# Attention weights of a graph layer: made ahead in four stages, with sums on ScalarE and a shorter ELU

## What is computed

```python
h = x @ W
al = h @ a_l
ar = h @ a_r
e = jnp.exp(-jax.nn.leaky_relu(al[src] + ar[dst], negative_slope=NEG_SLOPE))
rowsum = jax.ops.segment_sum(e, src, num_segments=N)
h_prime = jax.ops.segment_sum(e[:, None] * h[dst], src, num_segments=N)
h_prime = h_prime / (rowsum[:, None] + EPS)
return jax.nn.elu(h_prime)
```

## Time and profile before

| | us |
|---|---|
| median of three runs | 1708.2 |
| lowest, highest | 1707.59, 1710.76 |
| the profiled execution's own time | 1708.83 |
| its span in the profile | 1707.0 |
| PE busy | 1574.6 |
| DVE, ACT, POOL busy | 936.9, 720.7, 341.9 |

### The profile page before, as it was taken

The page is one execution under the profiler, slowest core; times in us unless marked ns, Lnnn a source line. Parts: engine busy times, 40 slices in busy tenths (PEclk is TensorE's granted clock), DMA queues, the critical chain, the costliest instruction groups (busy, mean ns, idle before and its releaser), DMA issues.

```text
span 1707.0 us, 19694 instructions
## 1 busy us (share of the span) xinstructions
PE 1574.6 (92%) x7072; PEld 1255.8 (74%) x7072; DVE 936.9 (55%) x1457; ACT 720.7 (42%) x1246; POOL 341.9 (20%) x670
## 2 busy tenths in 40 slices
PE   4797999999999999999999998978976999999995
PEld 3676778888677877787878777766754778777774
DVE  8785778887645343323342435554466538633345
ACT  4355766767733333333332233343322224543233
POOL 4132012233311010101010102232345104401015
PEclk9999999999999999999999999989988899999998
DMA  4233234324674434333444244533434145545235
GB/s 150 73 85 134 72 97 159 101 69 130 227 256 163 141 122 158 122 128 96 151 146 134 86 130 167 203 120 135 119 106 140 65 153 178 209 167 182 86 110 166
DMA packets 101882, 232.04 MB, mean 136 GB/s; under 512 B 22967, under 2 KB 25902, under 8 KB 101776
## 3 DMA queue, kind: packets, MB, share of 16 engines
q1 hardware_dynamic: 87366, 182.92, 33.7%
q10 hardware_dynamic: 14410, 47.74, 7.6%
HBM read 171.24 MB, written 59.37 MB: 135 GB/s over the span
## 4 chain that ended last, share of the span: by engine, by line
PE 63%; DVE 16%; ACT 8%; POOL 5%; issue 5%; DMA 2%; ACTq 0%; DVEq 0%; SPq 0%; POOLq 0%
PE bank L744 12%; PE bank L746 12%; PE bank L745 12%; PE bank L861 10%; PE bank L872 6%; PE bank L865 4%; PE bank L863 4%; ACT Tt L1007 2%; DMA x_d<-XO 2%; ACT Mh L987 1%; PE bank L795 1%; DVE Tt L1246 1%; ACT XO L1064 1%; PE bank L927 1%; DVE Ml L1232 1%
## 5 line engine op out<-in xcount | busy, mean ns | idle before, releaser
L744 PE MATMUL bank<-wh,xh 128*125 128x512 f32 x1040 | 423.1, 407 | 18.2 <-issue 14.3
L861 PE MATMUL bank<-Zh,Mh 125*125 125x512 f32 x1000 | 406.5, 406 | 8.4 <-ACT Mh L996 3.6
L745 PE MATMUL bank<-wl,xh 128*125 128x512 f32 x1040 | 412.7, 397 | 0.0
L746 PE MATMUL bank<-wh,xl 128*125 128x512 f32 x1040 | 412.4, 397 | 0.0
L1218 DVE TENSOR_TENSOR xl<-xs,xh 128x1000 fp32r<-128x1000 f32 x120 | 147.0, 1227 | 290.3 <-ACT xh L970 290.3
L970 ACT CAST xh<-xs 128x1000 fp32r<-128x1000 f32 x130 | 133.0, 1025 | 301.9 <-PE bank L746 284.2
L744 PEld LDWEIGHTS bank<-wh,xh 128*125 128x125 f32 x1040 | 194.7, 187 | 67.8 <-issue 16.8
L872 PE MATMUL bank<-Zl,Mh 125*125 125x512 f32 x600 | 237.6, 396 | 0.0
L746 PEld LDWEIGHTS bank<-wh,xl 128*125 128x125 f32 x1040 | 194.9, 187 | 49.9
L861 PEld LDWEIGHTS bank<-Zh,Mh 125*125 125x125 f32 x1000 | 189.9, 190 | 55.8 <-issue 6.2
L745 PEld LDWEIGHTS bank<-wl,xh 128*125 128x125 f32 x1040 | 195.1, 188 | 44.6
(11 more groups left out here) (165 smaller groups left out, 2110.6 us busy)
## 6 DMA issues: line engine op xcount, KB each, us to landing
xs<-xT_d SPq DMA_DIRECT2D x80, 500.0 KB, 3.6
Ar<-a_d SPq DMA_DIRECT2D x100, 312.5 KB, 3.1
xs<-hT_d SPq DMA_DIRECT2D x40, 500.0 KB, 3.6
x_d<-XO ACTq DMA_DIRECT2D x30, 512.0 KB, 4.0
R<-x_d SPq DMA_DIRECT2D x60, 256.0 KB, 4.2
xT_d<-XT ACTq DMA_DIRECT2D x30, 500.0 KB, 2.7
ws<-in_W SPq DMA_DIRECT2D x34, 256.0 KB, 3.3
m_d<-Tt ACTq DMA_DIRECT2D x10, 625.0 KB, 4.5
```

The lines of the kernel that those rows point to most:

```text
L744: te.matmul(o, xh[i % 2][:, k, :], wh[s][:], start=(k == 0), stop=False)
L745: te.matmul(o, xh[i % 2][:, k, :], wl[s][:], start=False, stop=False)
L746: m = te.matmul(o, xl[i % 2][:, k, :], wh[s][:], start=False, stop=(k == 7))
L861: te.matmul(o, Mh[i][:, s, :], zh, start=(n == 0), stop=False)
```

## The change

- **A third T tile.** Matrix d uses tile d mod 3. The third tile is laid over the two `XO` buffers, joined into one. `t_release` now takes the job that had the tile before.
- **Four stages.** For att job i, the sums and the leaky ReLU come at the end of iteration i - 4 (`SUM_AT`), the exponential and `times` in iteration i - 3 (`EXP_AT`), `Mh`, `Ml` and the fold in i - 2, the product in i. Its `Ar` is loaded in i - 4.
- **Sums on ACT** instead of POOL: ten activations of 125 x 125 with a column of `PQ` as bias.
- **Row sums.** One fold on POOL, to five blocks; PE sums five blocks instead of three, ahead of product j rather than behind it, into bank 6 or 7 by turns. `row_scale` makes `RS` early in DVE's iteration j.
- **ELU with one hop**, in att and kept jobs: ACT takes relu and exp of the scaled product straight from PSUM, DVE then takes min(exp, 1) + relu, and adds R and -1 as before. ACT thereby waits for the product's end itself, and for the `U` tiles.
- **The store to `m_d`** goes from ACT's queue to SP's, in `late(j)` for matrix j + 2, ahead of the load of `R` for j. For att and kept jobs DVE's `Ml` of j + 2 now comes after the layer norm's small step `soon` instead of before it; both are ahead of `post`.

```diff
+SUM_AT, EXP_AT = {}, {}
...
     if _j > J0[0] + 1:
-        LOAD_AT.setdefault(_j - 3, []).append(_j)
+        LOAD_AT.setdefault(_j - (4 if _job.kind == "att" else 3), []).append(_j)
+    if _job.kind == "att":
+        SUM_AT[_j - 4], EXP_AT[_j - 3] = _j, _j
+ATT = [_j for _j, _job in enumerate(JOBS) if _job.kind == "att"]
...
+def t_slot(j):
+
+    if JOBS[j].kind == "gate":
+        return TI[j] % 2
+    return JOBS[j].d % (3 if JOBS[j].kind == "att" else 2)
...
+T_BEFORE = {j: next((i for i in reversed(TJ[:TI[j]]) if t_slot(i) == t_slot(j)), None) for j in TJ}
...
-        XF = [sb(f"XO{i}", [128, D], f32) for i in range(2)]
+        XB = sb("XO", [128, 2 * D], f32)
+        XF = [XB[:, i * D:(i + 1) * D] for i in range(2)]
         XO = [t[0:T, :] for t in XF]
+
+        T3 = [TF[0][:], TF[1][:], XB[:, 0:NT * T]]
+        Tt.append(XB[0:T, 0:NT * T].rearrange("p (a c) -> p a c", c=T))
...
             q.wait_ge(s_ml, m_done(j))
             if JOBS[j].kind == "att":
-                q.wait_ge(s_half, 2 * JOBS[j].d + 2)
-                q.wait_ge(d_t[t_slot(j)], 16 * (JOBS[j].d // 2 + 1))
+                q.wait_ge(s_half, JOBS[j].d + 1)
+                m_stored(q, j)
+
+        def m_stored(q, j):
...
+            d = JOBS[j].d
+            q.wait_ge(d_m[d % 3], 16 * (d // 3 + 1))
...
+                if j + 2 < NJ and JOBS[j + 2].kind == "att":
+                    o = j + 2
+                    q.wait_ge(s_mul, e_done(o))
+                    sy.dma_start(m_d[JOBS[o].d], T3[t_slot(o)]).then_inc(d_m[JOBS[o].d % 3], 16)
...
-                if job.kind == "att":
-                    d = job.d
-                    q.wait_ge(s_half, 2 * d + 2)
-                    if d:
-                        q.wait_ge(s_post, PI[j])
-                    q.wait_ge(s_te, sum(1 for o in range(j) for _ in GROUPS[o]))
...
-                        m = te.matmul(bank[7][0:T, 0:1], GW[0:T, d % 2, c * T:(c + 1) * T], ones[0:T, 0:1],
-                                      start=(c == 0), stop=(c == 4))
-                    m.then_inc(s_row, 1)
+
+            def row_sums(j):
+                d = JOBS[j].d
+                q.wait_ge(s_half, d + 1)
+                if d >= 2:
+                    q.wait_ge(s_rs, d - 1)
+                q.wait_ge(s_te, 3 * NT + 1 + sum(1 for o in range(j) for _ in GROUPS[o]))
+                for c in range(NT // 2):
+                    m = te.matmul(bank[6 + d % 2][0:T, 0:1], GW[0:T, d % 2, c * T:(c + 1) * T], ones[0:T, 0:1],
+                                  start=(c == 0), stop=(c == NT // 2 - 1))
+                m.then_inc(s_row, 1)
...
-                if job.kind == "att":
-                    ac.dma_start(m_d[job.d], TF[t_slot(j)][:]).then_inc(d_t[t_slot(j)], 16)
...
+            def sums(j):
+
...
+                if t_slot(j) == 2 and d == 2:
+                    for o in range(NT - 2, NT):
+                        q.wait_ge(s_tt, GROUPS[fin_of(1, o)][-1][0] + 1)
+                        x_stored(q, fin_of(1, o))
+                else:
+                    t_release(q, T_BEFORE[j])
+                for s in range(NT):
+                    m = ac.activation(t[:, s, :], PB[:, d, :], ACT.Identity, bias=PQ[0][0][:, s:s + 1])
+                m.then_inc(s_sum, 1)
+
+            def exps(j):
+                q.wait_ge(s_leak, JOBS[j].d + 1)
+                ac.activation(Tt[t_slot(j)], Tt[t_slot(j)], ACT.Exp, scale=-1.0).then_inc(s_exp, 1)
...
                 elif job.kind in ("att", "kept"):
-                    q.wait_ge(s_el, NT * job.half + d + 1)
-                    ac.activation(U[1], U[1], ACT.Exp).then_inc(s_elu, 1)
+                    q.wait_ge(s_mm, j + 1)
+                    q.wait_ge(s_rs, d + 1)
+                    u_free(q, j)
+                    p = bank[BANK[j]][0:T, :]
+                    ac.activation(U[0], p, ACT.Relu, scale=RS[:, d:d + 1]).then_inc(s_elu, 1)
+                    ac.activation(U[1], p, ACT.Exp, scale=RS[:, d:d + 1]).then_inc(s_elu, 1)
...
+                if j in EXP_AT:
+                    exps(EXP_AT[j])
...
+                if j in SUM_AT:
+                    sums(SUM_AT[j])
...
+            def row_scale(j):
+                d = JOBS[j].d
+                q.wait_ge(s_row, 2 + d + 1)
+                chain("v", ve.tensor_scalar(RS[:, d:d + 1], bank[6 + d % 2][0:T, 0:1], 1e-5, None, ALU.add))
+                mine()
+                ve.reciprocal(RS[:, d:d + 1], RS[:, d:d + 1]).then_inc(s_rs, 1)
...
-                    q.wait_ge(s_mm, j + 1)
-                    u_free(j)
-                    chain("v", ve.tensor_scalar(U[0], p, RS[:, d:d + 1], None, ALU.mult))
-                    mine()
-                    ve.tensor_scalar(U[1], U[0], 0.0, None, ALU.min).then_inc(s_el, 1)
-                    q.wait_ge(s_elu, NT * f + d + 1)
-                    chain("v", ve.scalar_tensor_tensor(U[0], U[0], 0.0, U[1], ALU.max, ALU.add))
+                    q.wait_ge(s_elu, 2 * (NT * f + d) + 2)
+                    chain("v", ve.scalar_tensor_tensor(U[0], U[1], 1.0, U[0], ALU.min, ALU.add))
...
+                if j < NJ and JOBS[j].kind == "att":
+                    row_scale(j)
+                early = any(JOBS[i].kind in ("att", "kept") for i in FIRST_AT.get(j, []))
+                if early:
+                    lower(j)
+                if j in EXP_AT:
+                    times(EXP_AT[j])
...
+                if j in SUM_AT:
+                    leak(SUM_AT[j])
...
-                po.tensor_tensor(Tt[t_slot(j)], PB[:, job.d, :].unsqueeze(1).to_broadcast([T, NT, T]),
-                                 PQ[0][0][:, 0:NT].unsqueeze(2).to_broadcast([T, NT, T]), ALU.add).then_inc(s_add, 1)
...
-                q.wait_ge(s_half, 2 * d + 1)
-                po.tensor_tensor(s[:, 0:2, :], s[:, 0:2, :], s[:, 2:4, :], ALU.add).then_inc(s_half, 1)
```

More of the change, by code:

```diff
@@ L437, in gnn_program @@
         d_t = [sem(f"d_t{i}") for i in range(2)]
+        d_m = [sem(f"d_m{i}") for i in range(3)]
         d_r = [sem(f"d_r{i}") for i in range(4)]
@@ L563, in h_of, with u_free @@
             return next(j for j, job in enumerate(JOBS) if job.layer == 1 and job.second and (job.half, job.d) == (f, d))
+        def u_free(q, j):
+            prev = [o for o in PJ if o < j and (JOBS[o].kind in ("att", "kept", "loop") or JOBS[o].second)]
+            if len(prev) < 2:
+                for g in range(8, 16):
+                    if staging(g) > 5:
+                        slab_split(q, g)
+            for o in prev[-2:]:
+                if JOBS[o].layer == 1 and (o != prev[-1] or JOBS[j].layer != 1):
+                    q.wait_ge(s_tt, GROUPS[o][-1][0] + 1)
+                q.wait_ge(s_post, PI[o] + 1)
         def sync_program(_):
@@ L617, in load @@
                 if job.kind == "kept":
[L618 to L622, removed]
+                    t_release(q, T_BEFORE[j])
+                    m_stored(q, ATT[job.d])
+                    sy.dma_start(TF[t_slot(j)][:], m_d[job.d]).then_inc(d_t[t_slot(j)], 16)
                     return
@@ L1219, in second @@
                     return
-                if job.kind == "att":
-                    times(j)
                 i = MI[j]
@@ L1263, in edge, with leak, lower @@
                         .then_inc(s_diag, 1)
+            def leak(j):
+                t = Tt[t_slot(j)]
+                q.wait_ge(s_sum, JOBS[j].d + 1)
+                ve.scalar_tensor_tensor(t, t, 0.1, t, ALU.mult, ALU.max).then_inc(s_leak, 1)
+            def row_scale(j):
[4 more added lines that the diff above has]
+                ve.reciprocal(RS[:, d:d + 1], RS[:, d:d + 1]).then_inc(s_rs, 1)
+            def lower(j):
+                for i in FIRST_AT.get(j, []):
+                    if i in MSPLIT:
+                        second_part(i, EARLY)
+                    elif JOBS[i].kind in ("gate", "att", "kept"):
+                        second(i)
             def z_lower(i, n, src, scale):
@@ L1325, in after_apply @@
                                         op0=ALU.mult, op1=ALU.add, accum_out=PQ[0][0][:, d:d + 1]).then_inc(s_pq, 1)
-            def u_free(j):
-                prev = [o for o in PJ if o < j and (JOBS[o].kind in ("att", "kept", "loop") or JOBS[o].second)]
-                if len(prev) < 2:
-                    for g in range(8, 16):
-                        if staging(g) > 5:
-                            slab_split(q, g)
-                for o in prev[-2:]:
-                    if JOBS[o].layer == 1 and (o != prev[-1] or JOBS[j].layer != 1):
-                        q.wait_ge(s_tt, GROUPS[o][-1][0] + 1)
-                    q.wait_ge(s_post, PI[o] + 1)
             def post(j):
@@ L1586, in vector_program @@
                 for i in FIRST_AT.get(j, []):
-                    if JOBS[i].kind != "gate" and i not in (z0, z1):
+                    if JOBS[i].kind not in ("gate", "att", "kept") and i not in (z0, z1):
                         second(i)
@@ L1606, in vector_program @@
                     second_part(j + 1, REST)
```

(18 more changed lines are left out.)

48 lines of the change are left out of this document (20 added, 28 removed).

## The result

The changed kernel takes **1669.01 us** (median of 4 runs, 1665.94 to 1671.55) against 1709.48 for the kernel before on the same chip (4 runs, 1707.59 to 1712.94): a ratio of 0.976, 95% interval 0.9736 to 0.9784. It is faster, inside the range, and 6.5 us above the forecast of 1662.5.

The account below looks back on a forecast made before the run. TensorE was taken to lose time in the attention stage, waiting on a serial per-matrix chain at a lower clock: -32.0 waits, -16.2 clock, +2.1 row sums, net -46.1 from 1708.8, forecast 1662.5 us, range 1657 to 1676.

Parts of the forecast that it names:

- The attention stage: Ten attention products: TensorE sets the pace at 8.05 us each, 80.5 instead of 126.65, saving 46.1; 74%.
- ten sums at 3.0 us: ScalarE in the attention stage: ten small activations per matrix take 3.01 us; listed as a sign of being right.
- The row sums: TensorE, attention stage: five matmuls instead of three per group, 1.08 us a group.
- +2.1: Row sums in the attention stage: five matmuls at full clock for three, 10.8 less 8.7 us, added to the time.
- The helpers rival: Attention stage: VectorE, held by GpSimd, and ScalarE set the pace; loses 2 to 14 us, 1663 to 1673; 15%.
- The clock rival: Attention stage: small matmuls keep the clock near 0.81, stage 99.4 us, saving 27, total 1681.5; 5%.
- the slower one: Attention stage: SyncE's later load of R closes a loop; slower than before from a landing of 18.8 us; 4%.
- The DMA share of the stage: Attention stage: the same bytes in 80 us come to about 0.6 of the DMA engines, costed at nothing.
- The kept jobs: I take 0, with 1.5 either way: Kept jobs behind the attention stage: the shorter ELU changes nothing, 0 us, with 1.5 either way.
- The start: Start of the attention stage: first sums and exponentials fit into the last z iterations; the 3.1 us Zl wait goes.

Follow-up runs that it names:

- 5: The change with the ten attention sums back on GpSimd, one instruction per matrix: 1675.68 us, ratio 0.9786 to the kernel before.
- 9: The change with all ten row-sum groups in one PSUM bank, each waiting for the previous reciprocal: 1668.69 us, ratio 0.9744 to the kernel before.
- 10: The change with the attention matrices over two T tiles and not three: 1670.61 us, ratio 0.9745 to the kernel before.
- 11: The change with each attention matrix stored from ScalarE's queue, as in the kernel before: 1669.91 us, ratio 0.9743 to the kernel before.
- 4: The kernel before, old order kept, with row sums in bank 6 or 7 by turns: 1706.53 us, ratio 0.9978 to the kernel before.
- 3: The change with the second fold back on GpSimd and three row-sum matmuls instead of five: 1658.91 us, ratio 0.9711 to the kernel before.
- experiment 2: The change with the kept jobs' ELU in its old four steps, the new ELU only in attention jobs: 1669.24 us, ratio 0.9763 to the kernel before.
- 1: The changed kernel measured once more, unaltered, as yardstick: 1670.38 us, ratio 0.9765 to the kernel before.
- 6: The change with 88 idle one-column matmuls at the start, to shift TensorE's instruction fetches: 1667.28 us, ratio 0.9731 to the kernel before.
- 12: The change with 96 idle one-column matmuls at the start, a second shift of the fetches: 1663.73 us, ratio 0.974 to the kernel before.
- 8: The kernel of 3, with ScalarE's XT copies ahead of its ELU in the kept jobs: 1660.84 us, ratio 0.9701 to the kernel before.
- Experiment 7: The kernel of 3 with 40 idle one-column matmuls at the start: 1668.68 us, ratio 0.9737 to the kernel before.

## Why the prediction was right, and where its sum was off

- **The attention stage** (predicted 80.5, TensorE the largest): right to the hundredth, 80.51, in seven of the nine profiles with the new order and five row sums (5 and 9 are the other two). Waits gone, clock 1.00, ten sums at 3.0 us, each as said. The row sums took 1.01 us, not 1.08, and the products 7.04 instead of 6.97; that the two errors cancel is luck.
- **Which part does it.** Mostly the order of the stages, as far as taking parts away one at a time shows. The second bank is 0.9 us of it (9), the sums on ScalarE 3.8 (5), third tile and store queue nothing (10, 11), and the second bank alone in the old order 6.3 (4). That leaves some 40 of the 46.1 us; no kernel had the new order alone, and the attention jobs' shorter ELU, which frees VectorE, was not taken out.
- **The row sums.** Ten groups at 1.01 are 10.1 us where the prediction had 10.8, so its "+2.1" was 1.4. It took the loss as the price of making room on GpSimd. There was room: 19.48 busy of 80.5. At the full clock the two further matmuls of each group cost 4.4 us in all (3).
- **The helpers rival (15%)** did not occur in the change, where VectorE was busy for 64 us (6.4 for a product, 7.0 forecast) and ScalarE for 58.7 (5.9, not 7.4). What it rests on did: VectorE's last combining step takes 1.20 us on average beside GpSimd's fold, against 0.81 in the earlier trace rows. It only had time for that. It sets the pace one step away: with the sums on GpSimd (5) it costs 3.8 us. The clock rival and the slower one did not occur either; with the store ahead of `R` on SyncE's queue TensorE never waited in the stage. (The DMA share of the stage was worked out wrongly: 35.7% of 150 us is 0.67 of 80, not 0.6. Measured 0.62.)
- **"The kept jobs: I take 0, with 1.5 either way"** is the term that failed: +4.3. It looked for what the change does to the kept jobs' own instructions, found one hop less in the ELU, and experiment 2 confirms that this is worth nothing. The loss came from no edit there. Twenty more f32 matmuls in the stage moved the places where TensorE's instructions are fetched into the stores of two feature tiles, and those stores are on the path in the last kept jobs (a wait the prediction had seen, 3.9 us, without asking what ends it). The waits are 3.0 us longer, and 1.3 more is lost at the granted clock of 0.50 behind the longest of them.
- **The start** is 2.1 us later, where 0 was said. In 14 profiles the stage starts between 1217.55 and 1227.29; in the eight with five row sums and the sums on ScalarE (after; 1, 2, 6, 9 to 12), between 1218.41 (12) and 1225.39 (11). A shift of 2 us is inside that. Whether a part of it is the change's remains open.
- **The total**: 1662.5 + 4.3 + 2.1 + 0.4 outside the span gives 1669.3, against 1669.01 measured.

## What to carry to other kernels

A wait at a semaphore tells where lateness shows; give that wait what it asks for in the old order first (4), and see whether it moves on. When work is rebalanced, add it only to an engine that has time: one fold per matrix taken from a GpSimd with time to spare, in exchange for two matmuls, cost 4.4 us, and the kernels with the fold put back (3, 8) are the fastest of this study, 1658.91 and 1660.84 us. Experiment 7 has the same stage with other places of the fetches and took 1668.68. And where a stretch hangs on the landing of large stores, its time can move by 3 us with the number of instructions before it, so an edit is judged by its own stretch and by a shifted build, not by the total alone. A wait can cost more than its length: look at the granted clock behind it.

## What was not expected of the hardware

TensorE's instructions come in over the same DMA engines as the data. A packet of 16 KB that falls in a 512 KB store moves its landing from 3.5 to about 5.2 us, while TensorE itself waits in the kept jobs for nothing but the `XT` copies. The Trainium skill, "Runtime: NRT & Kernel Launch", section "Instruction fetch mechanics", says that instructions are fetched in blocks of 16 KiB, 256 instructions, by a DMA queue of the sequencer's own, at a cost that is mostly hidden. The block agrees: 80 more instructions brought the fetches 7 to 10 us earlier, some 80/256 of the 25 to 32 us between them, and 176 further ones brought them back to within 2 us. The cost is hidden from TensorE, but not from the store. The Trainium skill, "DMA: Bandwidth & Descriptors", section "Why a DMA increments its semaphore by 16 and not by 1", says that a transfer runs on up to 16 engines that finish independently and is complete only with the last. The trickle of 25 GB/s behind the store agrees with one engine that is late; which engine it was no view here shows.
